# The last batch of a two-layer kernel: second-layer products reordered by token half, expert stages drawn in among them, and eight subtractions moved from VectorE to GpSimd

## The reference

```
q, k, v  = x @ Wq, x @ Wk, x @ Wv
attn_out = softmax(q @ k^T * scale) @ v @ Wp + bp
cms_out  = gelu(attn_out @ cW1 + cb1) @ cW2 + cb2 + one_hot(code)
modifier = gelu([attn_out, cms_out] @ mW1 + mb1) @ mW2 + mb2
x        = clip(x + cms_out + modifier, 0, 1)
# expert e of each sequence
h        = gelu(x @ W_down[e] + b_down[e]) @ W_up[e] + b_up[e] + x
out      = layernorm(h) * ln_w[e] + ln_b[e]
```

## Time and profile before

| | us |
|---|---|
| median of three runs | 1093.36 |
| the profiled execution's own time | 1092.1 |
| its span, first to last instruction | 1090.3 |
| PE busy | 1052.4 (97%) |
| PE weight loads busy | 875.9 (80%) |
| DVE (VectorE) busy | 799.3 (73%) |
| ACT (ScalarE) busy | 513.1 (47%) |
| POOL (GpSimd) busy | 6.4 (1%) |
| mean granted TensorE clock | 0.997 |

### The profile page before, as it was taken

The page is one execution under the profiler, slowest core; times in us unless marked ns, Lnnn a source line. Parts: engine busy times, 40 slices in busy tenths (PEclk is TensorE's granted clock), DMA queues, the critical chain, the costliest instruction groups (busy, mean ns, idle before and its releaser), DMA issues. The chain is left out here.

```text
span 1090.3 us, 13978 instructions
## 1 busy us (share of the span) xinstructions
PE 1052.4 (97%) x4986; PEld 875.9 (80%) x4986; DVE 799.3 (73%) x1402; ACT 513.1 (47%) x913; POOL 6.4 (1%) x15
## 2 busy tenths in 40 slices
PE   8999999999999899999999999999999989999996
PEld 7889778888877688888789877888887767888885
DVE  4435986776587888877665698677667888877787
ACT  4425855444264443433565385544435534443462
POOL 0000000000000000000000000000000000000001
PEclk9999999999999999999999999999999999999999
DMA  5600121210243242312654122312013422332152
GB/s 198 228 1 16 68 73 39 78 39 20 78 147 104 78 154 78 115 41 94 253 163 103 46 77 78 116 39 78 20 63 131 136 78 103 130 135 69 33 151 78
DMA packets 54719, 101.61 MB, mean 93 GB/s; under 512 B 3103, under 2 KB 31867, under 8 KB 50811
## 3 DMA queue, kind: packets, MB, share of 16 engines
q1 hardware_dynamic: 54560, 100.70, 27.1%
q10 hardware_dynamic: 90, 0.02, 0.0%
HBM read 79.74 MB, written 20.97 MB: 92 GB/s over the span
## 5 line engine op out<-in xcount | busy, mean ns | idle before, releaser
L1042 DVE TENSOR_TENSOR acc<-bank,acc 128x512 f32<-128x512 f32 x224 | 154.1, 688 | 85.2 <-PE bank L218 85.0
L633 ACT ACTIVATE sbc<-sbc,bias 128x512 f32<-128x512 f32 x112 | 80.8, 724 | 268.1 <-DVE sbc L1012 202.9
L216 PE MATMUL bank<-hid_hi,w_lo 128*128 128x512 f32 x512 | 201.0, 393 | 4.6 <-DVE acc L1032 1.5
L217 PE MATMUL bank<-hid_hi,w_hi 128*128 128x512 f32 x512 | 199.5, 390 | 0.0
L218 PE MATMUL bank<-hid_lo,w_hi 128*128 128x512 f32 x512 | 199.5, 390 | 0.0
L216 PE MATMUL bank<-ta_hi,w_lo 128*128 128x512 f32 x448 | 175.9, 393 | 10.1 <-DVE sbc L1012 6.7
L218 PE MATMUL bank<-ta_lo,w_hi 128*128 128x512 f32 x448 | 174.4, 389 | 0.0
L217 PE MATMUL bank<-ta_hi,w_hi 128*128 128x512 f32 x448 | 174.4, 389 | 0.0
L1012 DVE TENSOR_TENSOR sbc<-bank,sbc 128x512 f32<-128x512 f32 x144 | 97.5, 685 | 31.9 <-PE bank L218 31.8
L216 PEld LDWEIGHTS bank<-hid_hi,w_lo 128*128 128x128 f32 x512 | 96.3, 188 | 29.6 <-DVE acc L1032 3.2
L218 PEld LDWEIGHTS bank<-hid_lo,w_hi 128*128 128x128 f32 x512 | 96.3, 188 | 20.1
(11 more groups left out here) (215 smaller groups left out, 1553.0 us busy)
## 6 DMA issues: line engine op xcount, KB each, us to landing
w_raw<-in_L_cond_mW SPq DMA_DIRECT2D x48, 512.0 KB, 3.6
w_raw<-in_L_cond_cW SPq DMA_DIRECT2D x32, 512.0 KB, 4.4
pre_d<-sbc SPq DMA_DIRECT2D x10, 1024.0 KB, 4.6
sbc<-pre_d SPq DMA_DIRECT2D x10, 1024.0 KB, 7.2
x_raw<-in_x SPq DMA_DIRECT2D x4, 1024.0 KB, 6.1
e_raw<-in_L_cond_W_down SPq DMA_DIRECT2D x8, 512.0 KB, 5.4
e_raw<-in_L_cond_W_up SPq DMA_DIRECT2D x8, 512.0 KB, 4.4
out<-acc SPq DMA_DIRECT2D x16, 256.0 KB, 2.1
```

The source lines that it names most:

```text
L216: nc.tensor.matmul(dst, w_l, a_h, start=start, stop=False, **kw)
L217: nc.tensor.matmul(dst, w_h, a_h, start=False, stop=False, **kw)
L633: nc.scalar.activation(dst, dst, ACT.Gelu, **kw).then_inc(g_done[key], 1)
L1042: nc.vector.tensor_tensor(dst, bank[:, :], dst, ALU.add).then_inc(evac, 1)
```

## The change

- The 24th quad's step stays the last of the loop in the last batch. What followed is written out for PE: l2(u,0), second 7, l2(u,1), l2(u,2), second 4, l2(u,3), second 3, l2(u,4), l2(u,5), l2(v,0) to (v,3), l2(u,6), (u,7), l2(v,4), (v,5), down(n), l2(v,6), (v,7), residual(n), up(n), down(n+1), residual(n+1), up(n+1). The tiles of the first token half are complete with l2(v,3).
- `group(r, k)` gives a group's place in that order; bank turns and the waits on `evac` and `l2_mm` go by it. `pe_up` is split into `pe_up_resid` and `pe_up`; batch 0 calls them one after the other, as before.
- Low parts of the last batch's eight pieces are subtracted by GpSimd (`pool_piece`, semaphore `q_l`) in the order 0 to 7. Pieces 0 to 5 stand ahead of GpSimd's power for the first half of norm(n), 6 and 7 between it and the second.
- ScalarE and VectorE get lists for the same order. VectorE clips each feature tile right behind its last evacuation. norm(n) is split: its first half stands before h3(n+1), its second behind it.
- SP waits on `q_l` for pieces 6 and 7, and on the new place of l2(u,7) for the last layer-norm rows.

```diff
+        LAST_L2 = ([(0, k) for k in range(6)] + [(1, k) for k in range(4)] + [(0, 6), (0, 7)]
+                   + [(1, k) for k in range(4, 8)])
+        def group(r, k):
+            r0 = RB * NBAT - 2
+            return 8 * r + k if r < r0 else 8 * r0 + LAST_L2.index((r - r0, k))
...
-                if 8 * (r - RB * b) + k >= 2:
-                    pe.wait_ge(evac, 8 * r + k - 1)
+                no = group(r, k)
+                if no - 8 * RB * b >= 2:
+                    pe.wait_ge(evac, no - 1)
...
+            if final:
+                u, v, n = QB - 2, QB - 1, 2 * b
+                l2(u, 0)
+                second(v, 7)
+                l2(u, 1)
+                l2(u, 2)
+                second(v, 4)
+                l2(u, 3)
+                second(v, 3)
+                l2(u, 4)
+                l2(u, 5)
+                for k in range(4):
+                    l2(v, k)
+                l2(u, 6)
+                l2(u, 7)
+                l2(v, 4)
+                l2(v, 5)
+                pe_down(pe, n)
+                l2(v, 6)
+                l2(v, 7)
+                pe_up_resid(pe, n)
+                pe_up(pe, n)
+                pe_down(pe, n + 1)
+                pe_up_resid(pe, n + 1)
+                pe_up(pe, n + 1)
...
-            pe_down(pe, 2 * NBAT - 2)
-            pe_down(pe, 2 * NBAT - 1)
-            pe_up(pe, 2 * NBAT - 2)
-            pe_up(pe, 2 * NBAT - 1)
...
+            act_expert_piece(act, b, 0)
+            act_expert_piece(act, b, 1)
+            act_xp(act, n)
+            act_expert_piece(act, b, 2)
+            act_expert_piece(act, b, 3)
+            act_up_bias(act, n)
+            act_down(act, n)
+            act_expert_piece(act, b, 4)
+            act_expert_piece(act, b, 5)
+            act_xp(act, n + 1)
+            act_expert_piece(act, b, 6)
+            act_expert_piece(act, b, 7)
+            act_up_bias(act, n + 1)
+            act_down(act, n + 1)
...
+            dve_evac(dve, b, u, 4)
+            dve_evac(dve, b, u, 5)
+            dve_hid(dve, b, v, "12")
+            for j in range(KT):
+                dve_evac(dve, b, v, j)
+                dve_clip(dve, n, (j,))
+            dve_evac(dve, b, u, 6)
+            dve_evac(dve, b, u, 7)
+            dve_xp(dve, n)
+            for j in (0, 1):
+                dve_evac(dve, b, v, KT + j)
+                dve_clip(dve, n + 1, (j,))
+            dve_h3(dve, n)
+            for j in (2, 3):
+                dve_evac(dve, b, v, KT + j)
+                dve_clip(dve, n + 1, (j,))
+            dve_xp(dve, n + 1)
+            dve_norm(dve, n, (0,))
+            dve_h3(dve, n + 1)
+            dve_norm(dve, n, (1,))
+            dve_norm(dve, n + 1)
...
+            for k in range(6):
+                pool_piece(pool, NBAT - 1, k)
+            pool_pow(pool, NB - 2, (0,))
+            for k in (6, 7):
+                pool_piece(pool, NBAT - 1, k)
+            pool_pow(pool, NB - 2, (1,))
+            pool_pow(pool, NB - 1)
...
+        def pool_piece(pool, bb, k):
+            pp, part, s = k // 4, k // 2 % 2, k % 2
+            hi, lo = (e_up if part else e_dn)[2 * bb + pp]
+            pool.wait_ge(e_h, 8 * bb + k + 1)
+            nc.gpsimd.tensor_tensor(lo[:, s, :], e_raw[E_STAGE[bb][k]][:, s, :], hi[:, s, :].bitcast(F32), ALU.subtract)\
+                .then_inc(q_l, 1)
```

More of the change, by code:

```diff
@@ L164, in build @@
         bu_in, xf_done, xb_done = sem("bu_in"), sem("xf_done"), sem("xb_done")
+        q_l = sem("q_l")
         w1_in = [sem(f"w1_in{s}") for s in range(2)]
@@ L211, in build @@
         E_LANDS = ((1, 1, 2, 2, 3, 3, 4, 4), (5, 5, 1, 1, 1, 1, 6, 6))
-        E_RANK = ((0, 1, 2, 3, 4, 5, 6, 7), (0, 1, 4, 5, 2, 3, 6, 7))
+        LAST_L2 = ([(0, k) for k in range(6)] + [(1, k) for k in range(4)] + [(0, 6), (0, 7)]
[3 more added lines that the diff above has]
+            return 8 * r + k if r < r0 else 8 * r0 + LAST_L2.index((r - r0, k))
         TILE = {"11": (0, 0, 0), "12": (0, 1, 1), "22": (1, 1, 2), "21": (1, 0, 3)}
@@ L385, in pe_attention @@
             if b:
+                pe_up_resid(pe, n - 2)
                 pe_up(pe, n - 2)
@@ L392, in pe_attention @@
             if b:
+                pe_up_resid(pe, n - 1)
                 pe_up(pe, n - 1)
@@ L411, in pe_down @@
                 for s in range(SEQ):
-                    pe.wait_ge(e_l, 8 * bb + E_RANK[bb][4 * pp + s] + 1)
+                    if bb + 1 < NBAT:
+                        pe.wait_ge(e_l, 8 * bb + 4 * pp + s + 1)
+                    else:
+                        pe.wait_ge(q_l, 4 * pp + s + 1)
                     for k in range(KT):
@@ L420, in pe_down, with pe_up_resid @@
                 last.then_inc(down_mm, 1)
-        def pe_up(pe, n):
-            bb, pp = divmod(n, 2)
+        def pe_up_resid(pe, n):
+            pp = n % 2
             b0 = 0 if pp else 4
-            (u_hi, u_lo), (t_hi3, t_lo3) = e_up[n], h3[n]
             for t in range(TT):
@@ L442, in pe_up @@
                                      start=k == 0, stop=True, skip_group_check=True)
+        def pe_up(pe, n):
+            bb, pp = divmod(n, 2)
+            b0 = 0 if pp else 4
+            (u_hi, u_lo), (t_hi3, t_lo3) = e_up[n], h3[n]
             pe.wait_ge(h3_l, 2 * n + 2)
@@ L445, in pe_up @@
                 s, tok = t // TS, slice(t * P, (t + 1) * P)
-                pe.wait_ge(e_l, 8 * bb + E_RANK[bb][4 * pp + 2 + s] + 1)
+                if bb + 1 < NBAT:
+                    pe.wait_ge(e_l, 8 * bb + 4 * pp + 2 + s + 1)
+                else:
+                    pe.wait_ge(q_l, 4 * pp + 2 + s + 1)
                 for m in range(MT):
@@ L523, in l2 @@
                     w = slice(j * P, (j + 1) * P)
-                    last = mm3(ps[6 + k % 2][:, :], w2_hi[reg][:, slot, c, w], w2_lo[reg][:, slot, c, w],
+                    last = mm3(ps[6 + no % 2][:, :], w2_hi[reg][:, slot, c, w], w2_lo[reg][:, slot, c, w],
                                hid_hi[reg][:, slot, c, t, :], hid_lo[reg][:, slot, c, t, :], c == 0, c == 1)
@@ L530, in pe_mlp @@
                 (first if which in (1, 2, 5, 6) else second)(i, which)
-            for it in range(2, QB + 2):
+            final = b + 1 == NBAT
+            for it in range(2, QB if final else QB + 2):
                 new, old, dn = it < QB, 2 <= it - 1 < QB, has_l2(it - 2)
@@ L796, in act_mlp @@
             cms_t = {10: ("B11", "B21"), 11: ("T1", "B22"), 12: ("T2", "T3"), 14: ("T4",)}
-            for it in range(QB + 2):
+            for it in range(QB + 2 if tail else QB):
                 new, old = it < QB, 0 <= it - 1 < QB
                 ph, pph = phase_of(it), phase_of(it - 1)
-                if not tail and it >= QB:
-                    for k in (0, 1) if it == QB else (4, 5):
-                        act_expert_piece(act, b, k)
                 if new and it > 1:
@@ L911, in act_expert_last @@
         def act_expert_last(act):
[L912 to L922, removed]
+            b = NBAT - 1
+            v, n = QB - 1, 2 * b
+            act_gelu(act, b, v, "22")
+            act_hid(act, b, v, "22")
+            act_w2(act, b, v)
+            for key in ("21", "12"):
+                act_gelu(act, b, v, key)
+                act_hid(act, b, v, key)
+            act_expert_piece(act, b, 0)
[12 more added lines that the diff above has]
+            act_down(act, n + 1)
         def act_program(act):
@@ L1024, in dve_evac @@
             t, j = divmod(k, KT)
-            bank = ps[6 + k % 2]
+            no = group(r, k)
+            bank = ps[6 + no % 2]
             dst = acc[:, j, t * TB:(t + 1) * TB]
-            dve.wait_ge(l2_mm, 8 * r + k + 1)
+            dve.wait_ge(l2_mm, no + 1)
             if r % RB == 0:
@@ L1034, in dve_evac @@
                 return
-            dve.wait_ge(evac, 8 * r + k - 7)
+            dve.wait_ge(evac, group(r - 1, k) + 1)
             if r % RB == NQ and k == 0:
@@ L1084, in dve_resid, with dve_clip @@
             nc.vector.tensor_tensor(dst, dst, xf[:, t, :, :], ALU.add).then_inc(resid_done, 1)
-        def dve_clip(dve, n):
+        def dve_clip(dve, n, tiles=range(4)):
             b, t = divmod(n, 2)
-            for j in range(KT):
-                dve.wait_ge(evac, 8 * (RB * b + RB - 1) + KT * t + j + 1)
+            for j in tiles:
+                dve.wait_ge(evac, group(RB * b + RB - 1, KT * t + j) + 1)
                 dst = acc[:, j, t * TB:(t + 1) * TB]
@@ L1129, in dve_expert_piece @@
             hi, lo = (e_up if part else e_dn)[2 * bb + pp]
-            dve.wait_ge(e_h, 8 * bb + E_RANK[bb][k] + 1)
+            dve.wait_ge(e_h, 8 * bb + k + 1)
             sub(lo[:, s, :], e_raw[E_STAGE[bb][k]][:, s, :], hi[:, s, :]).then_inc(e_l, 1)
@@ L1142, in dve_h3, with dve_norm @@
                 sub(h3[n][1][:, m, :], gel[n][:, m, :], h3[n][0][:, m, :]).then_inc(h3_l, 1)
-        def dve_norm(dve, n):
+        def dve_norm(dve, n, halves=(0, 1)):
             bb, pp = divmod(n, 2)
@@ L1149, in dve_norm @@
```

(49 more changed lines are left out.)

## The result

The changed kernel takes 1098.81 us (median of 7 runs, 1097.48 to 1099.36) against 1093.35 for the kernel before (7 runs): a ratio of 1.0047, 95% interval 1.0037 to 1.0057. It is 5.5 us slower, where 3.2 less was forecast; 1098.81 lies above the stated range.

What follows compares the result with a forecast made beforehand. PE was taken to bound the body, a relay ending on VectorE's norms the last 50 us. Half of norm(n) ahead of h3(n+1) gave 3.7 us less, minus 0.5 for margins: 1093.36 - 3.2 = 1090.2 us, range 1088.2 to 1096.5.

Steps and rivals of the forecast that it cites:

- The step that failed: Tail sums for VectorE and GpSimd: VectorE loses eight subtractions, 9.8 us; a GpSimd piece takes 2.3 us, powers not delayed.
- what makes the stalls go: Tail: taking eight subtractions of 1.22 us, 9.8 us in all, off VectorE removes PE's 3.58 us of stalls.
- Rival 2: Tail: VectorE's two-tile reads and clips wait for whole GpSimd instructions; 1.8 to 4.9 us slower; chance 0.30.
- the clean case: Tail runs as summed or nearly: 3.7 us less, 0.5 kept for margins, so 3.2 less; chance 0.46.
- three places: Where held VectorE delays PE: l2(v,3) 3.1 us late, down(n) 1.4 or 3.7 more, residual(n)'s third tile 1.8.
- the engines may share: Argument against VectorE being held: sharing would only lengthen GpSimd's pieces, with room up to 4.8 us each.
- its worst end: Holds on VectorE make PE 8.6 us late against 3.7 gained, 4.9 us slower; left out of the range.
- The likeliest case's low bound: Lower end of the clean case's own range, 1089.2 to 1092 us; its runs were put 1.5 to 4 us below before.
- The clean sum: End of the tail: h3(n+1), then 4.37 + 8.60 us of norms, ending at 1084.1 against 1087.76, 3.7 us less.
- The 0.5 us kept back for margins: Taken off the 3.7 us gain because VectorE's evacuations leave PE's next group small margins, 0.47 us.
- Rivals 3 and 4: 3: overlapping VectorE instructions stretch by tenths, 0 to 2 us less, chance 0.17; 4: GpSimd pieces 4.8 us or more, 0.07.
- SP, DMAs, ScalarE: Tail: transfers cost nothing, up to 10 us late for pieces 6 and 7; ScalarE no longer delays down(n+1).

Runs made afterwards that it cites:

- low_parts_on_vector: Changed kernel with all eight low-part subtractions back on VectorE, pieces 0 and 1 one loop step earlier: 1089.85 us against 1092.51 for the kernel before, ratio 0.9972.
- the phases above: Kernel before plus short phases behind its end, GpSimd beside four VectorE instructions: two-tile reads 2.49 us beside a memset, 4.65 beside a copy; clips 3.48 beside a memset.
- norm_in_one_block: low_parts_on_vector with the first half of norm(n) put back behind h3(n+1): 1093.74 us against 1093.18 for the kernel before, ratio 1.0007.
- gpsimd_timed: Changed kernel with two more GpSimd waits, pieces 2 and 4 starting after the low parts of xp(n) and xp(n+1): 1092.03 us against 1092.51 before, ratio 0.9996.
- all seven kernels of the table: Kernel before, changed kernel and five follow-up variants of who subtracts, when, or where norm(n) stands; the six changed ones measured 1088.90 to 1098.81 us.
- the first experiments: Those measured beside the kernel before at 1092.51 us: low_parts_on_vector 1089.85, the old order with GpSimd subtracting 1096.66, gpsimd_timed 1092.03.

## Why the prediction was wrong

- **The step that failed** is the one under **VectorE** and **GpSimd**: GpSimd's price was taken as its own duration alone, 2.3 us for a piece, and VectorE's other instructions were left at their lengths of before, so the holds were a term at nothing in the sum. The duration was right (2.34 to 2.35 alone, 2.4 to 2.6 in the kernel). What was missing is what it costs VectorE: about 2.15 us for each instruction that meets it (2.83 against 0.68), 4.0 for the four of xp(n), and 9.4 us on PE's path, 1.6 of them by the clock.
- **A second step was wrong** and did no harm to the number: that the eight subtractions taken from VectorE are "what makes the stalls go". low_parts_on_vector keeps them all on VectorE, and PE has no stall. The move that cost the time was not needed.
- **The weights.** Rival 2 had this mechanism with its three places and was given 0.30 against 0.46 for the clean case. Its worked-out 3.1, 3.7 and 1.8 us were 3.69, 3.95 and 1.75. The trace of before had the hint (a clip at nearly twice the pace of an evacuation). Against it stood only that the engines may share, and no row showed that either; an absent row is no evidence for the side that costs nothing. The Trainium skill (SBUF, Who interferes with whom) says this of both forms, down to the memset that leaves two-tile readers alone, and the phases above agree with it at each point (2.49, 3.48, 4.65 us). With the hint in the rows it deserved more weight than the clean case.
- **The size of rival 2.** 8.6 us of stalls at most were worked out and 9.4 came. By cause: the evacuations behind the held hidden part and clip cost 2.95 for 3.1, the waits for xp(n) 3.05 (0.74 and 2.31) for 3.7, residual(n)'s third tile 1.75 for 1.8; the 1.64 of down(n)'s fallen clock had no term. So even its worst end, 1098.3, was 0.5 too low, and the range was cut at 1096.5. (The likeliest case's low bound, 1089.2, is 1089.4 by its own 4 us; nothing hangs on it.)
- **The clean sum was right for the order.** 3.7 us less, with down(n+1) 46.43 us behind l2(u,0) and 12.97 behind h3(n+1), is what low_parts_on_vector shows in its tail (-3.69, 46.40, and 12.97 from 1072.96 to 1085.93). The medians give 2.7 for it, and 3.6 to 3.7 at like clock. The 0.5 us kept back for margins was not needed: PE had no idle bracket.
- **Where the gain sits.** That half of norm(n) is the gain (4.26 us) was right: norm_in_one_block loses 4.28.
- **Rivals 3 and 4.** Partial stretching shows nowhere: an instruction that meets GpSimd waits to the end of GpSimd's, and the next ones have their usual length. A slow GpSimd was not the cause: PE never waited for a piece, and starting them later made the tail 6.5 us shorter.
- **SP, DMAs, ScalarE.** Nothing was late there, as predicted.

## What to carry to other kernels

Before work is moved to GpSimd, list what VectorE does in the same microseconds: in these runs each VectorE instruction of two SBUF inputs waited to the end of a GpSimd instruction that read SBUF, and each tensor_scalar on one SBUF tile to the end of any, even a memset, while those that read PSUM and at most one tile ran on. If it must be moved, put it behind a semaphore into a stretch where VectorE reads PSUM or has slack; two such waits took back 6.5 us. And ask first whether it must be moved: here VectorE had the room elsewhere in its list. Where the engine that sets the end works off a block at the end of a relay, the gain lies in what can be taken ahead of its last input, and here the sum for it, made from before's rows, came within 0.1 us of the tail.

## What was not expected of the hardware

- A held instruction is shown as busy. A small instruction is held like a large one: in gpsimd_timed the norm's addition on two columns (line 1210, 0.17 us elsewhere) lasts 1.82 us beside piece 5, in its VectorE timeline:

```profile
1063.88 1.82 DVE L1210 TENSOR_SCALAR veps<-mv 128x2 f32<-128x2 f32 x1
```

- The two engines take turns. Four queued subtractions don't stay together when GpSimd has a second instruction waiting: both pieces of a pair hold VectorE, with one instruction in between (6.47 and 6.41 us; the first two matmul groups of down(n), at 1048.79 and 1051.46, are released 2.67 us apart).
- The same idle stretch of PE is not always followed by the same clock. At the turn of the batches PE is idle for 2.19 us (2.20 in one) in the profiles of all seven kernels of the table. In six the next stretch is granted in full, in low_parts_on_vector it is not. The code of the two is the same there. The windows view of the kernel before, columns as above:

```profile
530.00:535.00 5.00, 4.93 (x22) 4.08 (x23) 5.00 (x11) 5.00 (x11) 0.00 (x0) 1.00 0.53 223
```

The same view of low_parts_on_vector:

```profile
530.00:535.00 5.00, 4.78 (x14) 3.80 (x15) 5.00 (x11) 5.00 (x11) 0.00 (x0) 0.66 0.59 251
```

In 375 to 380 us, where PE was idle for 1.9 us before the first matmul at 375.70, the kernel before itself has a fallen clock:

```profile
375.00:380.00 5.00, 4.30 (x12) 3.20 (x13) 3.04 (x5) 4.35 (x9) 0.00 (x0) 0.66 0.01 3
```

The same view of gpsimd_timed, with the same 1.90 us of idle time before it:

```profile
375.00:380.00 5.00, 4.19 (x17) 3.22 (x18) 3.04 (x7) 4.56 (x9) 0.00 (x0) 1.00 0.02 3
```

Of the seven profiles four have 0.66 or 0.67 there and three 1.00.

The execution of low_parts_on_vector starts l2(u,0) at 1024.15, where before starts it at 1022.26: 1.9 us for a cause outside the change, 1.74 of them behind the idle stretch at 530. The spread between runs goes with the clock: of 21 runs of the kernel before beside the first experiments, the ten with a mean granted clock of 0.997 or more took 1091.82 to 1092.58 us, the seven with 0.995 or less 1093.38 to 1095.32. What decides whether the clock falls stays open. For a change in the tail the tail's length in the profile was the sharper measure: it gave 64.35 us for two kernels whose medians differ by 0.95. But it is one execution of each kernel.
